# A pairwise-interaction tower: the short block of z on both halves of the rows, beside 64-row products, and a new order of the pieces

## The chip, the core and the metric

The kernel runs on one core of a Trainium2 chip. The metric is the device time in microseconds (us) of one execution, the median of several runs. All data are float32.

## What is computed

2048 samples, 32 features each. Each feature id picks a row of 64 numbers from its own table, so a sample has x of 32 x 64. From it come 32 row sums and 496 pair values x_i K_ij x_j, which with 16 dense numbers enter three dense layers.

```python
def _L0_rec_ref(x, kernels):
    ...
    z = jnp.sum(x, axis=-1)
    xi = x[:, II, :]
    xj = x[:, JJ, :]
    outer = jnp.einsum('bpd,pde,bpe->bp', xi, kernels, xj)
    return jnp.concatenate([z, outer], axis=1)
...
e = jnp.stack([tbl_0[ids[:, 0]], tbl_1[ids[:, 1]], ...], axis=1)
z = _L0_rec_ref(e, L0_rec_kernels)
h = jnp.concatenate([z, dense_ctx], axis=1)
h = jnp.maximum(h @ W_top1 + b_top1, 0.0)
h = jnp.maximum(h @ W_top2 + b_top2, 0.0)
y = h @ W_top3
```

## The kernel before, in words

The samples are cut into 8 batches (q = 0 to 7) of 256, two tiles of 128. Two features make a stage, so there are 16 stages; stage a holds one feature in the upper 64 rows and one in the lower 64 rows of `x_t`. These two halves of the rows of TensorE's array are called sides here: side 0 is rows 0 to 63, side 1 is rows 64 to 127.

A batch has 64 steps, in the order of `STEPS`. A step fills one of three product buffers `m_ps` (`MR = 3`) in PSUM and is then multiplied by VectorE. There are two kinds, 32 of each:

- An even step E0 to E31 (`multiply`, lines 633 and 635): four matmuls, two per side, with 64 rows of K as weights and 256 samples moving. VectorE's product (line 475) goes to `prod`. After every second even step TensorE adds up the products of an earlier pair with `sel` (`reduce`, line 663).
- A turned step T0 to T31 (`multiply_turned`, line 649): one matmul per side, with x as weights and 512 columns of K moving. VectorE's product (line 500) goes to `turned_act` or `turned_dve`; the sums over 64 are then made by ScalarE (line 409, sixteen small instructions a step) or, for the steps in `BY_VECTOR`, by VectorE itself (line 508, one instruction).

A step may begin when the product three steps earlier is finished (`prod_ready`). The last matmul of a step signals `step_done`, for which VectorE waits.

Between the steps TensorE does the pieces of the tower, each of them placed ahead of or behind an even step by the hand-written table `PLACED`, and each through the one buffer `tr` in PSUM: ScalarE must have copied a piece out (`tr_kept`) before the next may fill `tr`. The pieces of a batch are: "x" (line 553), eight transposes of two stages each for the next batch or for later stages of the same one; "xsum" (line 559), the transposes of the 32 row sums; "t" (line 567), those of the turned sums; "h1" 0 to 3 (line 572), the four chunks of the first layer; "h2" 0 and 1 (line 586), the second; and "y" (line 594), the third. Chunks belong to the batch before the one in whose steps they stand. The fifth number of a row in `PLACED` says how many steps later ScalarE copies the piece.

A chunk of h1 is five matmuls over the blocks of z: two of even pairs, two of turned pairs, and the short block (`ZSHORT`), of whose 128 rows only 48 carry values: 32 row sums and 16 dense numbers.

GpSimd gathers the table rows (line 310), four gathers a stage, and from batch 1 on also adds the two halves of each gathered row (`halve`, line 293), four gathers behind. A transposition "x" waits for that (`x_halved`), since `gathered` and `x_half` are rings.

In the last batch h1 is computed in the product buffers instead (`layer1_of_last`).

Of the kernel before, what the change touches and what calls it, by code (L numbers as in the profile page):

```python
# [20 lines left out]
MR = 3  # L21
# [24 lines left out]
BY_VECTOR = [_i in (1, 5, 6, 10, 12, 16, 18, 21, 23, 26, 28, 30) for _i in range(NT)]  # L46
# [5 lines left out]
for _a in range(STAGES):  # L52
# [6 lines left out]
    if _a % COLS == COLS - 1:  # L59
# [29 lines left out]
for _what, _i in STEPS[0]:  # L89
# [13 lines left out]

QUADS_OF_BLOCK = 16
# [7 lines left out]
ZLAST = SUM_ROWS + DENSE  # L112

# [71 lines left out]
VECTOR_SUMS_BEHIND = (1, 3, 5, 6, 7, 8, 9, 12, 13, 16, 17, 22, 25, 31)  # L185


def dlrm_tower(nc, ids, tables, kmat, dense_t, w1, b1, w2, b2, w3, out):
# [6 lines left out]
    with ctx:  # L195
# [122 lines left out]
        def _(sp):  # L318
# [14 lines left out]
            for q in range(NQ):  # L333
# [3 lines left out]
                sp.dma_start(z_sb[SUM_ROWS:ZLAST, q % 2, ZSHORT, :], dense_t[:, q * QB:(q + 1) * QB]).then_inc(dense_loaded[q % 2], 16)  # L337
# [8 lines left out]
        def _(act):  # L346
# [188 lines left out]
        def _(pe):  # L535
# [20 lines left out]
            def sums_of_x(q):  # L556
                pe.wait_ge(x_summed, (q + 1) * STAGES)
                for t in range(TILES):
                    last = nc.tensor.transpose(tr[0:SUM_ROWS, 0, t * P:(t + 1) * P], z_nat[:, q % 2, t, :], ident[:])
                last.then_inc(tr_filled, 1)  # L560

            def sums_of_turned(q):
# [5 lines left out]
                last.then_inc(tr_filled, 1)  # L568

# [28 lines left out]
            def fill(what, q, n):  # L598
# [3 lines left out]
                free_tr(what, q, n)  # L602
# [176 lines left out]
```

## Time and profile before

| | |
|---|---|
| median of 3 runs | 815.76 us (815.51 to 815.84) |
| the profiled execution, its own time | 816.48 us |
| its span, first to last instruction | 814.7 us |
| TensorE busy | 768.5 us (94%) |
| VectorE busy | 722.7 us (89%) |
| ScalarE busy | 682.0 us (84%) |
| GpSimd busy | 607.1 us (75%) |
| DMA engines, mean of the last 36 of 40 slices | one tenth or less |

The profile was taken in one execution. PE is TensorE's matmuls, PEld its weight loads, DVE VectorE, ACT ScalarE, POOL GpSimd. A float32 matmul of the program stands as two passes in the rows, so an even step has eight rows, a turned step four, a chunk of h1 ten. The time of a piece of TensorE's work is read here from the start of its first row to the start of the first row of the next piece, since the rows' own ends overlap.

### The profile page before, as it was taken

How to read it: one execution, taken by the hardware profiler on the slowest of the kernel's cores; microseconds unless marked ns; L12 is line 12 of the kernel's file. 1: busy time of each engine (PE TensorE's matmuls, PEld its weight loads, DVE VectorE, ACT ScalarE, POOL GpSimd, SP SyncE). 2: the span in 40 equal slices, each digit the busy share in tenths (PEclk: the TensorE clock that was granted, in tenths of full speed). 3: DMA queues.
4: the chain of work that ended last, by engine and by line, in shares of the span. 5: the costliest groups of instructions: out<-in, count | busy, mean ns of one | idle time of the engine just before them, and what ended most of it. 6: DMA issues, size and time to landing. Idle time of an engine off the chain costs nothing.

```text
span 814.7 us, 20371 instructions
## 1 busy us (share of the span) xinstructions
PE 768.5 (94%) x6000; PEld 451.0 (55%) x6000; DVE 722.7 (89%) x684; ACT 682.0 (84%) x5282; POOL 607.1 (75%) x966
## 2 busy tenths in 40 slices
PE   0389989999999999999999999999999999999998
PEld 0245445565655655565556556555565656565556
DVE  0269999989999899989999899999999899998992
ACT  1049897899879997899888998799978998889983
POOL 6776888888888887888868887888868888682000
PEclk9889999999999999999999999999999999999999
DMA  4545111111111111111111111111111111110000
GB/s 135 162 148 166 27 26 24 26 24 26 25 27 25 24 26 21 27 25 24 26 20 24 26 23 23 25 24 26 24 21 25 25 25 26 20 25 8 1 2 1
DMA packets 20014, 28.74 MB, mean 35 GB/s; under 512 B 9024, under 2 KB 9664, under 8 KB 19008
## 3 DMA queue, kind: packets, MB, share of 16 engines
q0 software_dynamic: 16384, 16.81, 10.7%
q1 hardware_dynamic: 3520, 10.63, 3.9%
q8 instruction: 48, 0.79, 0.4%
q14 instruction: 62, 0.51, 0.2%
HBM read 27.40 MB, written 0.01 MB: 34 GB/s over the span
## 4 chain that ended last, share of the span: by engine, by line
PE 79%; POOL 8%; DMA 6%; issue 3%; DVE 2%; ACT 1%; DVEq 0%; POOLq 0%
PE m_ps L649 24%; PE m_ps L633 24%; PE acc L663 13%; PE tr L572 8%; POOL gathered L310 7%; DMA gathered<-in_tbl,idx 6%; PE tr L553 4%; PE tr L586 3%; PE m_ps L572 1%; DVE prod L475 1%; POOL x_half L293 1%; ACT turned_act L409 1%; PE m_ps L635 1%; DVE turned_act L500 1%; PE tr L567 0%
## 5 line engine op out<-in xcount | busy, mean ns | idle before, releaser
L409 ACT ACTIVATE turned_act<-turned_act 128x64 f32<-128x64 f32 x2560 | 611.9, 244 | 2.7 <-DVE turned_act L500 2.6
L310 POOL DMA_INDIRECT gathered<-in_tbl,idx x512 | 489.4, 956 | 101.1 <-issue 76.6
L409 ACT ACTIVATION_READ_ACCUMULATOR turned_act<-turned_act 128x1 f32 x2560 | 488.3, 191 | 0.0
L475 DVE TENSOR_TENSOR prod<-m_ps,x_t 128x1024 f32<-128x1024 f32 x256 | 307.5, 1214 | 21.2 <-PE m_ps L635 20.3
L633 PE MATMUL m_ps<-x_t,k_sb 64*128 64x256 f32 x1024 | 269.1, 389 | 4.2 <-DVE turned_dve L500 2.6
L635 PE MATMUL m_ps<-x_t,k_sb 64*128 64x256 f32 x1024 | 269.4, 390 | 0.0
L649 PE MATMUL m_ps<-k_sb,x_t 64*128 64x512 f32 x1024 | 257.1, 609 | 1.3 <-DVE turned_dve L500 0.7
L633 PEld LDWEIGHTS m_ps<-x_t,k_sb 64*128 64x128 f32 x1024 | 184.4, 188 | 112.4 <-issue 73.7
L500 DVE TENSOR_TENSOR turned_act<-m_ps,gathered 128x1024 f32<-128x1024 f32 x160 | 192.5, 1215 | 13.9 <-PE m_ps L649 6.0
L635 PEld LDWEIGHTS m_ps<-x_t,k_sb 64*128 64x128 f32 x1024 | 184.2, 188 | 0.0
L293 POOL TENSOR_TENSOR x_half<-gathered 128x32 f32<-128x32 f32 x448 | 117.1, 262 | 30.0 <-DVE z_nat L459 20.8
L663 PE MATMUL acc<-prod,sel 128*32 128x256 f32 x2048 | 138.1, 387 | 0.6 <-DVE prod L475 0.5
L649 PEld LDWEIGHTS m_ps<-k_sb,x_t 64*128 64x128 f32 x1024 | 90.8, 186 | 74.5 <-issue 62.9
L500 DVE TENSOR_TENSOR turned_dve<-m_ps,gathered 128x1024 f32<-128x1024 f32 x96 | 117.1, 1219 | 7.8 <-issue 2.4
L508 DVE TENSOR_REDUCE z_turned<-turned_dve 128x16 f32<-128x1024 f32 x96 | 115.9, 1208 | 0.0
L353 ACT ACTIVATE x_t<-tr 128x512 f32<-128x512 f32 (+1 forms) x72 | 39.2, 545 | 69.5 <-PE tr L553 68.9
L663 PEld LDWEIGHTS acc<-prod,sel 128*32 128x32 f32 x2048 | 53.5, 109 | 66.1 <-issue 26.3
L553 PE MATMUL tr<-ident,gathered 128*128 128x128 f32 x256 | 45.0, 294 | 36.4 <-DMA gathered<-in_tbl,idx 34.7
L572 PE MATMUL tr<-z_sb,w_sb 128*128 128x256 f32 x280 | 67.9, 389 | 0.0
L553 PEld LDWEIGHTS tr<-ident,gathered 128*128 128x128 f32 x256 | 27.2, 143 | 66.2 <-issue 31.5
L572 PEld LDWEIGHTS tr<-z_sb,w_sb 128*128 128x128 f32 x280 | 50.9, 190 | 19.7 <-issue 14.0
L450 DVE TENSOR_REDUCE z_nat<-gathered 128x4 f32<-128x256 f32 x16 | 6.6, 412 | 32.1 <-DMA gathered<-in_tbl,idx 32.1
(36 smaller groups left out, 152.8 us busy)
## 6 DMA issues: line engine op xcount, KB each, us to landing
gathered<-in_tbl,idx POOLq DMA_INDIRECT x512, 2.5
k_sb<-in_kmat SPq DMA_DIRECT2D x7, 1024.0 KB, 4.9
w_sb<-in_w SPq DMA_DIRECT2D x1, 1280.0 KB, 9.0
k_sb<-in_kmat SPq DMA_DIRECT2D x2, 256.0 KB, 3.2
k_sb<-in_kmat SPq DMA_DIRECT2D x1, 512.0 KB, 5.0
w_sb<-in_w SPq DMA_DIRECT2D x1, 512.0 KB, 10.9
idx<-in_ids SPq DMA_DIRECT2D x1, 256.0 KB, 2.7
z_sb<-in_dense_t SPq DMA_DIRECT2D x8, 16.0 KB, 1.8
```

The source lines that it names most:

```text
L293: nc.gpsimd.tensor_tensor(x_half[:, G % HR, t, f, :], at[:, 0:D // 2], at[:, D // 2:D], ALU.add).then_inc(x_halved, 1)
L310: nc.gpsimd.indirect_dma_start(out=gathered[:, t, G % GR, f * D:(f + 1) * D], out_offset=None, in_=tables[2 * (STAGES - 1 - a) + f], in_of ...
L409: last = nc.scalar.activation(row, row, ACT.Copy, accum_out=z_turned[:, q % 2, t, 16 * c + n:16 * c + n + 1])
L475: nc.vector.tensor_tensor(prod[:, r % PR, :, :].rearrange("p u (e n) -> p u e n", e=2), m_ps[:, p % MR, :, :].rearrange("p u (e n) -> p u ...
L500: nc.vector.tensor_tensor(to, m_ps[:, p % MR, :, :], other, ALU.mult).then_inc(prod_ready, 1)
L508: nc.vector.tensor_reduce(z_turned[:, q % 2, t, 16 * c:16 * c + 16], turned_dve[:, (q * NTD + RANK[i]) % BD, :, :].rearrange("p f (u n) -> ...
L553: last = nc.tensor.transpose(tr[:, c, t * P:(t + 1) * P], gathered[:, t, (G + c) % GR, :], ident[:])
L572: last = nc.tensor.matmul(to, w1_sb[:, b, n * P:(n + 1) * P], z_sb[:, q % 2, b, :], start=(begin and b == blocks[0]), stop=(end and b == b ...
L633: nc.tensor.matmul(m_ps[:, p % MR, 0, n * QB:(n + 1) * QB], k_sb[0:D, at + n, :], x_t[0:D, slot(q, a0), :], start=True, stop=True)
L635: last = nc.tensor.matmul(m_ps[:, p % MR, 1, n * QB:(n + 1) * QB], k_sb[D:P, at + n, :], x_t[D:P, slot(q, a1), :], start=True, stop=True)
L649: last = nc.tensor.matmul(m_ps[:, p % MR, f, :], x_t[f * D:(f + 1) * D, slot(q, m), t * P:(t + 1) * P], k_sb[f * D:(f + 1) * D, at:at + CO ...
L663: last = nc.tensor.matmul(acc[c * 32:c * 32 + 32, 0:QB], sel[:, 30 - 2 * row:62 - 2 * row], prod[:, (q * NE + e) % PR, u, n * QB:(n + 1) * ...
```

## The change

The short block of z and its weights are put on both sides: rows 0 to 47 and rows 64 to 111 hold the same. The dense numbers are loaded twice, "xsum" gets for each tile a second matmul that writes the 32 sums to rows 64 to 95, and ScalarE copies them with a second instruction. A chunk's short block becomes one 64-row matmul (`short_block`), on side 0 for chunks 0 and 2, where it comes last, and on side 1 for chunks 1 and 3, where it comes first (`open_chunk`) and is issued ahead of the reduction that stands before the rest of the chunk. Between the two, the steps issue side 1 first (`sides = (1, 0)`).

In the last batch the short blocks of the four chunks are issued one behind the other, on alternate sides.

The order is new: both tables of turned steps, the places of all pieces and their copies, 13 instead of 12 turned steps summed by VectorE, and where those sums stand.

```diff
-BY_VECTOR = [_i in (1, 5, 6, 10, 12, 16, 18, 21, 23, 26, 28, 30) for _i in range(NT)]
+BY_VECTOR = [_i in (1, 4, 6, 9, 13, 15, 16, 18, 20, 23, 25, 29, 31) for _i in range(NT)]
...
-TURNED_LATER = [0, 1, 3, 5, 5, 7, 8, 8, 9, 11, 11, 11, 12, 12, 14, 14, 15, 16, 16, 17, 17, 20, 21, 22, 22, 24, 24,
+TURNED_LATER = [1, 1, 1, 2, 3, 5, 5, 6, 8, 8, 9, 12, 12, 13, 14, 14, 16, 16, 18, 18, 18, 19, 21, 21, 22, 24, 24,
...
-    ("x", 8, BEHIND, 5, 1),
+    ("x", 8, BEHIND, 3, 1),
...
-    ("xsum", 0, AHEAD, -3, 0),
+    ("xsum", 0, AHEAD, -4, 1),
-    ("h1", 0, BEHIND, 9, 2),
-    ("h1", 1, AHEAD, 12, 1),
-    ("h1", 2, AHEAD, 14, 2),
-    ("h1", 3, BEHIND, 17, 0),
+    ("h1", 0, BEHIND, 5, 4),
+    ("h1", 1, BEHIND, 7, 3),
+    ("h1", 2, BEHIND, 15, 1),
+    ("h1", 3, BEHIND, 17, -1),
...
-                sp.dma_start(z_sb[SUM_ROWS:ZLAST, q % 2, ZSHORT, :], dense_t[:, q * QB:(q + 1) * QB]).then_inc(dense_loaded[q % 2], 16)
+                for side in (0, D):
+                    sp.dma_start(z_sb[side + SUM_ROWS:side + ZLAST, q % 2, ZSHORT, :], dense_t[:, q * QB:(q + 1) * QB]).then_inc(dense_loaded[q % 2], 16)
...
+                nc.scalar.activation(z_sb[D:D + SUM_ROWS, q % 2, ZSHORT, :], tr[D:D + SUM_ROWS, 0, :], ACT.Copy).then_inc(tr_kept, 1)
...
+                    last = nc.tensor.matmul(tr[D:D + SUM_ROWS, 0, t * P:(t + 1) * P], z_nat[:, q % 2, t, :], ident[:], start=True, stop=True)
...
+            def short_block(q, n, to, begin, end):
+                side = D * (n % 2)
+                return nc.tensor.matmul(to, w1_sb[side:side + D, ZSHORT, n * P:(n + 1) * P], z_sb[side:side + D, q % 2, ZSHORT, :],
+                                        start=begin, stop=end)
+
+            def open_chunk(what, q, n):
+                free_tr(what, q, n)
+                short_block(q, n, tr[:, 0, :], True, False)
...
-                    layer1(q, n, tr[:, 0, :], range(NZ), True, True).then_inc(tr_filled, 1)
+                    if n % 2 == 0:
+                        layer1(q, n, tr[:, 0, :], range(ZSHORT), True, False)
+                        short_block(q, n, tr[:, 0, :], False, True).then_inc(tr_filled, 1)
+                    else:
+                        layer1(q, n, tr[:, 0, :], range(ZSHORT), False, True).then_inc(tr_filled, 1)
...
+                        sides = (1, 0) if what[0] == "h1" and what[2] % 2 == 0 else (0, 1)
...
-            layer1_of_last((NB - 1, ZSHORT), False, False)
+            layer1_of_last((NB - 1,), False, False)
+            for n in range(H1 // P):
+                short_block(LAST, n, m_ps[:, n // 2, n % 2, 0:QB], False, False)
```

What stands in a row on TensorE around chunks 0 and 1 of a batch in the middle, before (the lines' names are those of the list above; `acc` is a reduction, `tr<-z_sb` a chunk; an even step is four rows of 633 and 635):

```order
L663 MATMUL acc<-prod,sel 32x256 x8
L572 MATMUL tr<-z_sb,w_sb 128x256 x5
L649 MATMUL m_ps<-k_sb,x_t 128x512 x2
L633 MATMUL m_ps<-x_t,k_sb 128x256
L635 MATMUL m_ps<-x_t,k_sb 128x256
...
L663 MATMUL acc<-prod,sel 32x256 x8
L553 MATMUL tr<-ident,gathered 128x128 x4
L649 MATMUL m_ps<-k_sb,x_t 128x512 x6
L572 MATMUL tr<-z_sb,w_sb 128x256 x5
```

The same place after the change, where line 589 is the four full blocks of a chunk, 580 a short block, 670 turned steps (two matmuls each), 656 even steps (four each) and 684 a reduction:

```order
L684 MATMUL acc<-prod,sel 32x256 x8
L589 MATMUL tr<-z_sb,w_sb 128x256 x4
L580 MATMUL tr<-z_sb,w_sb 128x256
L670 MATMUL m_ps<-k_sb,x_t 128x512 x4
L656 MATMUL m_ps<-x_t,k_sb 128x256 x4
L670 MATMUL m_ps<-k_sb,x_t 128x512 x2
L656 MATMUL m_ps<-x_t,k_sb 128x256 x4
L580 MATMUL tr<-z_sb,w_sb 128x256
L684 MATMUL acc<-prod,sel 32x256 x8
L589 MATMUL tr<-z_sb,w_sb 128x256 x4
```

Between the two short blocks stand five steps (T5, T6, E6, T7, E7). Chunks 2 and 3 stand in the same way around four steps (E16, T16, T17, E17).

On VectorE the run of five steps that stood between a reduction and the next one before, T5, E8, T6, T7, E9, and its sums:

```order
L500 TENSOR_TENSOR turned_dve<-m_ps,gathered 128x1024
L475 TENSOR_TENSOR prod<-m_ps,x_t 128x1024
L508 TENSOR_REDUCE z_turned<-turned_dve 128x16
L500 TENSOR_TENSOR turned_dve<-m_ps,gathered 128x1024
L500 TENSOR_TENSOR turned_act<-m_ps,gathered 128x1024
L475 TENSOR_TENSOR prod<-m_ps,x_t 128x1024
```

And VectorE's rows for the run between the short blocks of chunks 0 and 1 after the change: T5, T6, E6, the sum of T6, T7, E7 and E8 (507 is a turned product, 482 an even one, 515 a turned sum):

```order
L507 TENSOR_TENSOR turned_act<-m_ps,gathered 128x1024
L507 TENSOR_TENSOR turned_dve<-m_ps,gathered 128x1024
L482 TENSOR_TENSOR prod<-m_ps,x_t 128x1024
L515 TENSOR_REDUCE z_turned<-turned_dve 128x16
L507 TENSOR_TENSOR turned_act<-m_ps,gathered 128x1024
L482 TENSOR_TENSOR prod<-m_ps,x_t 128x1024 x2
```

The two turned products have moved together to the head of the run.

The third place is the start of a batch on TensorE, up to "x" 8, the transposition of stages 8 and 9. Before, where the first row is "x" 4 of that batch, nine steps and three reductions stand ahead of the last row (rows of even steps are left out):

```order
L553 MATMUL tr<-ident,gathered 128x128 x4
L633 MATMUL m_ps<-x_t,k_sb 128x256
L635 MATMUL m_ps<-x_t,k_sb 128x256
...
L649 MATMUL m_ps<-k_sb,x_t 128x512 x2
...
L663 MATMUL acc<-prod,sel 32x256 x8
L553 MATMUL tr<-ident,gathered 128x128 x4
L649 MATMUL m_ps<-k_sb,x_t 128x512 x2
...
L663 MATMUL acc<-prod,sel 32x256 x8
L567 MATMUL tr<-ident,z_turned 128x128 x4
...
L663 MATMUL acc<-prod,sel 32x256 x8
L553 MATMUL tr<-ident,gathered 128x128 x4
```

After (560 is "x", 575 is "t"):

```order
L656 MATMUL m_ps<-x_t,k_sb 128x256 x8
L684 MATMUL acc<-prod,sel 32x256 x8
L560 MATMUL tr<-ident,gathered 128x128 x4
L670 MATMUL m_ps<-k_sb,x_t 128x512 x6
L575 MATMUL tr<-ident,z_turned 128x128 x4
L656 MATMUL m_ps<-x_t,k_sb 128x256 x4
L670 MATMUL m_ps<-k_sb,x_t 128x512 x2
L656 MATMUL m_ps<-x_t,k_sb 128x256 x4
L684 MATMUL acc<-prod,sel 32x256 x8
L560 MATMUL tr<-ident,gathered 128x128 x4
```

Eight steps and two reductions now stand ahead of "x" 8, one of each fewer.

## Rows read from the trace of the kernel before

**Rows 1.** Stretches between two times, busy us (instructions) of each engine:

```profile
core 0: us, PE busy (x) PEld busy (x) DVE busy (x) ACT busy (x) POOL busy (x), PEclk, DMA share, GB/s
324.88:419.46 94.58, 94.58 (x751) 56.17 (x750) 89.88 (x85) 84.82 (x660) 77.99 (x129) 1.00 0.13 24
132.80:230.31 97.51, 95.13 (x753) 55.97 (x749) 91.54 (x86) 85.89 (x672) 85.11 (x140) 1.00 0.13 25
...
148.26:230.31 82.05, 82.05 (x635) 48.51 (x635) 76.77 (x72) 75.35 (x592) 71.63 (x117) 1.00 0.13 26
```

**Rows 2.** Chain that ended last, 159 to 265 us: start us, us, what:

```profile
159.21 2.36 PE tr L572 x10
...
206.10 1.92 PE tr L586 x8
...
252.79 1.00 PE acc L663 x16
253.79 2.36 PE tr L572 x10
...
259.94 0.59 PE tr L553 x4
```

**Rows 3.** Timeline of TensorE around a run of five steps: start us, us, instruction:

```profile
342.65 1.13 PE L649 MATMUL m_ps<-k_sb,x_t 64*128 64x512 f32 x4
343.61 0.38 PE L633 MATMUL m_ps<-x_t,k_sb 64*128 64x256 f32 x1
343.62 0.38 PE L635 MATMUL m_ps<-x_t,k_sb 64*128 64x256 f32 x1
343.83 0.38 PE L633 MATMUL m_ps<-x_t,k_sb 64*128 64x256 f32 x1
...
344.48 1.88 PE L649 MATMUL m_ps<-k_sb,x_t 64*128 64x512 f32 x8
346.24 0.48 PE L633 MATMUL m_ps<-x_t,k_sb 64*128 64x256 f32 x1
...
347.30 1.07 PE L663 MATMUL acc<-prod,sel 128*32 128x256 f32 x16
```

**Rows 4.** Timeline of VectorE for the same five steps:

```profile
343.83 1.23 DVE L500 TENSOR_TENSOR turned_dve<-m_ps,gathered 128x1024 f32<-128x1024 f32 x1
344.97 1.21 DVE L475 TENSOR_TENSOR prod<-m_ps,x_t 128x1024 f32<-128x1024 f32 x1
```

**Rows 5.** Timeline of TensorE around "y" and "xsum":

```profile
406.46 1.07 PE L663 MATMUL acc<-prod,sel 128*32 128x256 f32 x16
407.35 0.41 PE L594 MATMUL tr<-h_sb,w_sb 128*1 128x64 f32 x16
...
410.47 0.39 PE L559 MATMUL tr<-ident,z_nat 128*32 128x128 f32 x2
410.79 0.48 PE L633 MATMUL m_ps<-x_t,k_sb 64*128 64x256 f32 x1
```

**Rows 6.** Timeline of TensorE in batch 1, idle time before in brackets:

```profile
146.00 1.07 PE L663 MATMUL acc<-prod,sel 128*32 128x256 f32 x16
148.26 0.66 PE L553 MATMUL tr<-ident,gathered 128*128 128x128 f32 x4 [1.19 <-POOL x_half L293]
```

**Rows 7.** Timeline of TensorE in batch 3, its "x" 8:

```profile
337.42 0.66 PE L553 MATMUL tr<-ident,gathered 128*128 128x128 f32 x4
```

**Rows 8.** Timeline of VectorE in batch 0:

```profile
45.52 1.23 DVE L475 TENSOR_TENSOR prod<-m_ps,x_t 128x1024 f32<-128x1024 f32 x1 [2.42 <-PE m_ps L635]
49.20 1.23 DVE L500 TENSOR_TENSOR turned_act<-m_ps,gathered 128x1024 f32<-128x1024 f32 x1 [2.46 <-DMA gathered<-in_tbl,idx]
```

**Rows 9.** Timeline of TensorE in the tail, the first 24 of the last chunks' passes:

```profile
798.58 5.35 PE L572 MATMUL m_ps<-z_sb,w_sb 128*128 128x256 f32 x24
```

**Rows 10.** Waits of POOL, 132.8 to 703.2 us: total us, times, longest:

```profile
POOL x_half L293 <- DVE z_nat L459: 20.8, 5, 4.9
```

**Rows 11.** Groups of instructions, ACT, 132.8 to 703.2 us: busy us, mean ns | idle before:

```profile
L409 ACT ACTIVATE turned_act<-turned_act 128x64 f32<-128x64 f32 x1927 | 460.5, 244 | 0.0
L371 ACT ACTIVATE z_sb<-tr 32x256 f32<-32x256 f32 x6 | 2.1, 358 | 0.0
```

More of the change, by code:

```diff
@@ L112 @@
 ZLAST = SUM_ROWS + DENSE
+assert ZLAST <= D
 K_LOADS = [4, 4, 8] + [16] * 7
@@ L632, in multiply, with multiply_turned @@
                 for n, (a0, a1, _, _) in enumerate(EVEN[e]):
-                    nc.tensor.matmul(m_ps[:, p % MR, 0, n * QB:(n + 1) * QB], k_sb[0:D, at + n, :], x_t[0:D, slot(q, a0), :],
-                                     start=True, stop=True)
-                    last = nc.tensor.matmul(m_ps[:, p % MR, 1, n * QB:(n + 1) * QB], k_sb[D:P, at + n, :], x_t[D:P, slot(q, a1), :],
-                                            start=True, stop=True)
+                    for f in sides:
+                        last = nc.tensor.matmul(m_ps[:, p % MR, f, n * QB:(n + 1) * QB], k_sb[f * D:(f + 1) * D, at + n, :],
+                                                x_t[f * D:(f + 1) * D, slot(q, (a0, a1)[f]), :], start=True, stop=True)
                 last.then_inc(step_done, 1)
-            def multiply_turned(q, i):
+            def multiply_turned(q, i, sides):
                 c, t = divmod(i, TILES)
@@ L667, in reduce @@
                         last.then_inc(reduced, 1)
+            sides = (0, 1)
+            opened = set()
             for q in range(NQ):
@@ L671, in _ @@
                     if kind == "turned":
-                        multiply_turned(q, n)
+                        multiply_turned(q, n, sides)
                         continue
-                    for what in AHEAD.get((q, n), ()):
+                    ahead, behind = AHEAD.get((q, n), ()), BEHIND.get((q, n), ())
+                    for what in ahead:
+                        if what[0] == "h1" and what[2] % 2:
+                            open_chunk(*what)
                         fill(*what)
-                    multiply(q, n)
+                        sides = (1, 0) if what[0] == "h1" and what[2] % 2 == 0 else (0, 1)
+                    multiply(q, n, sides)
+                    if behind and behind[0][0] == "h1" and behind[0][2] % 2:
+                        open_chunk(*behind[0])
+                        opened.add(behind[0])
                     if n % GROUP == GROUP - 1:
+                        sides = (0, 1)
                         if n >= GROUP:
@@ L681, in _ @@
                             reduce(q - 1, NG - 1)
-                    for what in BEHIND.get((q, n), ()):
+                    for what in behind:
+                        if what[0] == "h1" and what[2] % 2 and what not in opened:
+                            open_chunk(*what)
                         fill(*what)
+                        sides = (1, 0) if what[0] == "h1" and what[2] % 2 == 0 else (0, 1)
             reduce(LAST, NG - 1)
```

49 lines of the change are left out of this document (26 added, 23 removed).

## The prediction, written before the result was known

> **What bounds the kernel now.** I read the stretches first. In batch 3, from 324.88 to 419.46 us, TensorE is busy for all 94.58 us, VectorE for 89.88, ScalarE for 84.82, GpSimd for 77.99, all at the full clock [rows 1]. The chain that ended last says the same: it is a list of TensorE's pieces, and chunk 0 of h1 returns in it after 253.79 - 159.21 = 94.58 us [rows 2]. So from batch 2 on the period is the sum of what stands in TensorE's queue. Batch 1 is the exception: it takes 97.51 us of which TensorE is busy for 95.13 [rows 1], and the largest hole is the 1.19 us ahead of its "x" 8, which waits for GpSimd's halves [rows 6]; from there to the end of the batch the 82.05 us are dense again [rows 1]. Batch 0 is set by landing gathers and then by VectorE.
>
> Four prices for TensorE come out of the starts of the rows. A chunk of five blocks takes 2.36 us, h2 with four such matmuls 1.92 or so: a full block is 0.43 [rows 2]. A step is 0.86 (343.61 to 344.48; two in 344.48 to 346.24 with a little more) [rows 3]. The first step behind other work takes 0.96 (342.65 to 343.61), so entering a run of 64-row steps costs 0.10 [rows 3]; I take leaving it as 0.10 too, since a reduction of four passes deep lasts 1.00 [rows 2] where its passes fill 0.86. And the two sides run beside each other: line 633 starts at 343.61, line 635 at 343.62, and the second pass of 633 only at 343.83 [rows 3].
>
> VectorE is near enough to matter. A product follows another after 1.14 us (343.83 to 344.97) [rows 4], so in an unbroken run of steps TensorE, at 0.86 each, gains 0.28 a step on it and may be three steps ahead. A product begins 1.18 after the first row of its step (342.65 to 343.83). E9 was the fifth step of such a run and needed the product of E8, which ended at 344.97 + 1.21 = 346.18; E9 began at 346.24, where two turned steps end at 346.20, and had to pay the entry again (its first row is 0.48 instead of 0.38) [rows 3, 4]. So one such stop costs 0.04 to 0.10 plus 0.10. There are three a batch (E9, E17, E23), together some 0.55 us.
>
> **The change in a middle batch.** (1) Four full blocks go, 4 x 0.43 = 1.73 us. (2) Four 64-row matmuls of 0.43 come. If one on side 0 opens a run, the steps start on side 1, and one on side 1 closes it, both sides have the same load and a pair costs one slot: 2 x 0.43 = +0.85. Together -0.88.
>
> (3) "xsum" grows by two ordinary matmuls with 128 moving columns, two passes of half of 0.21 each, 0.43 in all. "y", sixteen passes on four groups of columns, takes 0.34 [rows 5], so different groups of columns do run side by side, and the transposes and the new matmuls write to different ones. No row shows the two kinds mixed. Bounds: +0.2 when they overlap ("xsum" is 0.32 now, 410.47 to 410.79 [rows 5]), +0.43 one behind the other, +0.7 if each change of kind costs an entry. I take +0.3, nearer to "y".
>
> (4) The number of runs of 64-row work goes from 19 to 20 a batch: +0.20. "y" no longer stands behind a reduction, where the reduction took 0.89 (406.46 to 407.35) [rows 5] instead of 1.00: +0.11; "xsum" now does and may get the same back. Net +0.06.
>
> (5) The old stops go, -0.55, and new ones come. In the run between chunks 0 and 1 the steps are issued side 1 first, so the last matmul of each step, which signals `step_done`, is on the side that carries the short block, and is 0.43 late. Count from the short block, with the entry 0.10: T5 starts at 0.10, T6 0.96, E6 1.82, T7 2.68, E7 3.54. VectorE gets T5 at 0.10 + 1.08 + 0.43 = 1.61, ends it at 2.83 and releases T7 0.06 later, at 2.89: a stop of 0.21. T6's product starts at 2.75, ends 3.96, frees E7 at 4.02, while TensorE is ready at 2.89 + 0.10 + 0.86 = 3.85: a stop of 0.17. With an entry each that is 0.58. The run between chunks 2 and 3 has four steps, E17 meets the first stop again: 0.31. E15, the fifth of a run without the delay, stops as E9 did: 0.16. New stops: 1.05. VectorE can't be ahead here: ahead of T5 it has waited for a reduction and four full blocks, about 2.9 us, and one more turned sum per batch (1.13 us) is spent where it has room: 94.58 - 89.88 = 4.7 us.
>
> Sum: 94.58 - 0.88 + 0.30 + 0.20 + 0.06 - 0.55 + 1.05 = **94.76 us**, +0.18 a batch. With the ends of (3) and (4) it is 94.6 to 95.3.
>
> ScalarE is given nothing that shows: it loses one turned step (sixteen times 244 ns [rows 11], in part overlapped), and gets one copy of about 358 ns [rows 11] a batch. The second dense load is a 16 KB transfer once a batch that waits for the same event as the first and is needed some twenty steps later. GpSimd waits for VectorE's sums up to 4.9 us in a batch now [rows 10], which is its slack; "x" 14 moves three even steps forward, so that wait moves with it. It would bind only under 94.58 - 4.9 = 89.7 us a batch.
>
> **Batch 0 and 1.** In batch 0 E2 moves behind the landing of stage 6. Before, VectorE had E3's product at 45.52 and then waited until 49.20 for stage 7 [rows 8]; now E2 fills that hole and E3 is left for later, and there is one turned sum more: batch 1 starts about 2 x 1.13 = 2.3 us later, at some 135.1. That is covered. "x" 8 of batch 1 can't run before 148.26 [rows 6], since GpSimd's gathers run without a break up to there and nothing moves them. TensorE now needs 10.7 us from the start of the batch to that point (before 337.42 - 324.88 = 12.5 in an undisturbed batch [rows 1, 7], less one step, 0.86, and one reduction, 1.00): it gets there at 145.8 and waits. But the step and the reduction that don't stand ahead of this wait any more have to be done behind it. From 148.26 to the end of the batch it takes 94.76 - 10.7 = 84.1 instead of 82.05 [rows 1]: **+2.0 us**, once.
>
> **Tail.** The 24 passes from 798.58 on [rows 9] lead the end. Four full short blocks become four 64-row ones in two slots: -0.85, and +0.20 for entering and leaving: -0.65.
>
> Total: +2.0 + 6 x 0.18 - 0.65 = +2.4. Batch 7 has the same steps and counts as one of the six. Against the profiled execution, 814.7 span and 816.48 in all, this is 818.9; the median lies 0.7 lower, so 815.76 + 2.4 = 818.2. I forecast **818.2 us**. In general the result is 815.8 + 7 x (P - 94.41), with P the period: 0.35 us of P decide over the sign.
>
> **Rivals.** A: the delay of 0.43 is not felt, because both sides of a step end together or the product is ready anyway. Then of the new stops only E7 and E15 stay as E9 was, 0.3 instead of 1.05: P = 94.0, 813.0 us. For it: the three stops before are only 0.04 to 0.10 deep. Against: the two sides start freely of each other [rows 3], and a queue of equal loads keeps its offset to the end of the run. Chance 0.22.
>
> B, slower: the short blocks don't hide. A product that starts alone on side 1 has to wait for the whole of the short block; the place is the head and the end of each of the two runs, the price up to 4 x 0.43 = 1.7 instead of 0.85 a batch, less 0.75 for stops that vanish with the offset: P between 94.9 and 95.6, 819 to 824 us. It decides as soon as more than 0.2 of each 0.43 is exposed. Against it stand the starts 0.01 apart of 633 and 635 [rows 3]. Chance 0.1.
>
> B2, slower: the passes start in the program's order, so that the first product on side 1 starts with the second pass of the short block, 0.21 behind its first. Half of each short block is exposed, 2 x 0.21 more a batch, while the offset and with it the stops shrink by about 0.2: P about 95.0, 820 us. Against it: the first pass of line 635 starts 0.21 ahead of the second pass of 633 [rows 3], although the program issues both passes of 633 in one matmul ahead of it. Chance 0.05. The Trainium skill, TensorE: Matmul & The Clock Gate, Part 3, What overlaps and what doesn't, says that matmuls start strictly in program order and that only weight loads are pulled ahead; by that rule this rival is what happens, and the trace of before does not agree.
>
> C: "xsum" at its dearest and every stop 0.1 deeper: P = 95.3, 822 us. Chance 0.08.
>
> D: the term of batch 1 is absent, because something between "x" 8 and the end of that batch has slack I don't see: 816.2 us. Against: 82.05 of 82.05 us busy. Chance 0.07.
>
> E: the change does not do what it says in its order, that is a copy by ScalarE (places of the fifth column) is late and TensorE waits for `tr`, 0.5 us a batch: 821 us. ScalarE idles 10 us a batch, so chance 0.05.
>
> My own forecast, P within 94.5 to 95.0, 816.5 to 820, has 0.43.
>
> **Range and chances.** 813.2 to 822.5 holds all but the ends of A, B and C. A measurement of this kernel tells 0.2% from no change, so the bounds are 814.1 and 817.4. Faster: most of A, 0.2. Same: the rest of A, D and the lower end of mine, 0.24. Slower: 0.56.
>
> **What will show it.** Right if the row after a chunk's four full blocks shows the short block and the first product of side 1 within 0.01 us of each other; if the period is 94.5 to 95.0 with stops ahead of T7, E7 and E17 and none ahead of E9 and E23; if "x" 8 of batch 1 still starts at 148.2 to 148.4 with an idle of 2 to 3 us before it, and the batch behind it takes 84 us; if "xsum" takes 0.5 to 0.75; and if the last chunks take 0.65 less. Wrong if no stop stands at T7 and E17 (A), if the first product starts 0.2 or more behind the short block (B or B2), or if batch 2 begins less than 1 us later than before (230.31).

## The result: 824.67 us, 8.9 us more than before

The changed kernel takes 824.67 us (median of 4 runs, 824.3 to 826.42), the kernel before 815.77 in the same comparison: a ratio of 1.0109, 95% interval 1.0097 to 1.0121. The direction was forecast, the size was not: 818.2 us was said, with a range up to 822.5. The profiled execution has a span of 822.6 us and 824.38 in all, 7.9 more than that of before (814.7 and 816.48).

Stretches of the changed kernel between the starts of its batches, busy us of each engine; they answer to [rows 1]:

```profile
core 0: us, PE busy (x) PEld busy (x) DVE busy (x) ACT busy (x) POOL busy (x), PEclk, DMA share, GB/s
135.67:233.00 97.33, 95.63 (x758) 56.52 (x754) 90.59 (x86) 81.03 (x626) 85.10 (x139) 1.00 0.13 25
148.11:233.00 84.89, 84.89 (x666) 50.46 (x666) 78.15 (x74) 72.33 (x562) 74.13 (x121) 1.00 0.13 25
328.56:424.11 95.55, 95.55 (x758) 56.53 (x755) 90.42 (x86) 81.43 (x630) 82.81 (x136) 1.00 0.13 26
```

TensorE is still the bound and still dense, but a middle batch takes 95.55 us instead of 94.58, and from "x" 8 of batch 1 to the end of that batch it takes 84.89 instead of 82.05. No other engine has moved near: VectorE has 90.42 of 95.55, GpSimd 82.81. So 7.9 us of span are: batch 2 begins at 233.00 instead of 230.31 (+2.69), five batches at +0.97 (+4.9), batch 7 +0.8, tail -0.5.

"xsum" in the timeline of TensorE of the changed kernel (start, length, line, operation), to be held against [rows 5], where it took 0.32 us:

```profile
507.06 1.07 PE L684 MATMUL acc<-prod,sel 128*32 128x256 f32 x16
508.06 0.29 PE L566 MATMUL tr<-ident,z_nat 128*32 128x128 f32 x1
508.28 0.41 PE L567 MATMUL tr<-ident,z_nat 128*32 128x128 f32 x2
508.62 0.28 PE L566 MATMUL tr<-ident,z_nat 128*32 128x128 f32 x1
508.83 0.41 PE L567 MATMUL tr<-ident,z_nat 128*32 128x128 f32 x2
509.17 0.49 PE L656 MATMUL m_ps<-x_t,k_sb 64*128 64x256 f32 x2
```

Line 566 is the transpose to rows 0 to 31, line 567 the new ordinary matmul to rows 64 to 95. They never run beside each other: an ordinary matmul starts 0.21 to 0.22 behind the transpose before it, the second transpose 0.34 behind the first of the two passes of the matmul before it, and the whole takes 509.17 - 508.06 = 1.10 us (the profile's own rounding), 0.78 more than before.

The run between chunks 0 and 1 of h1, TensorE and then VectorE:

```profile
345.52 0.48 PE L580 MATMUL tr<-z_sb,w_sb 64*128 64x256 f32 x1
345.53 0.69 PE L670 MATMUL m_ps<-k_sb,x_t 64*128 64x512 f32 x1
345.84 0.38 PE L580 MATMUL tr<-z_sb,w_sb 64*128 64x256 f32 x1
...
347.35 1.23 PE L656 MATMUL m_ps<-x_t,k_sb 64*128 64x256 f32 x7
348.39 0.69 PE L670 MATMUL m_ps<-k_sb,x_t 64*128 64x512 f32 x1
...
349.52 1.13 PE L656 MATMUL m_ps<-x_t,k_sb 64*128 64x256 f32 x8
350.49 0.59 PE L580 MATMUL tr<-z_sb,w_sb 64*128 64x256 f32 x2
...
```

```profile
347.11 1.23 DVE L507 TENSOR_TENSOR turned_act<-m_ps,gathered 128x1024 f32<-128x1024 f32 x1 [0.81 <-PE m_ps L670]
348.25 1.22 DVE L507 TENSOR_TENSOR turned_dve<-m_ps,gathered 128x1024 f32<-128x1024 f32 x1
...
```

The short block (line 580) and the first matmul of T5 (line 670) start 0.01 apart, so it is hidden. Its price is the lag: VectorE begins T5's product at 347.11, 1.58 after the first row instead of the 1.18 of [rows 3, 4]. T7 starts at 348.39, where E6, begun at 347.35, leaves one side free after 0.86, at 348.21: a stop of 0.18. E7 starts at 349.52, where T7 with its entry of 0.10 would be done at 349.35: 0.17. Each of the two waits for the product three steps earlier: T5's product ends at 347.11 + 1.23 = 348.34, 0.05 before T7 starts, and T6's at 348.25 + 1.22 = 349.47, 0.05 before E7.

Batch 1 of the changed kernel around "x" 8, and the first 24 passes of the last chunks, which answer to [rows 6] and [rows 9]:

```profile
145.34 1.07 PE L684 MATMUL acc<-prod,sel 128*32 128x256 f32 x16
148.11 0.66 PE L560 MATMUL tr<-ident,gathered 128*128 128x128 f32 x4 [1.70 <-POOL x_half L298]
...
806.99 3.62 PE L589 MATMUL m_ps<-z_sb,w_sb 128*128 128x256 f32 x16
810.54 1.13 PE L580 MATMUL m_ps<-z_sb,w_sb 64*128 64x256 f32 x8
811.60 0.44 PE L598 MATMUL tr<-ident,z_turned 128*128 128x128 f32 x2
```

"x" 8 is still tied to GpSimd, at 148.11 instead of 148.26. The 24 passes last from 806.99 to 810.54 + 1.13 = 811.67, 4.68 us where they were 5.35. From their first row to the start of the next piece it is 811.60 - 806.99 = 4.61 us, where it was 803.76 - 798.58 = 5.18, so 0.57 less.

### The profile page after: what moved, and what is told of

It is laid out like the page before. It is cut to its first block, busy times and chain, and to the rows that moved or that the text cites. A ratio compares the mean times of both kernels' runs of the same rounds, so it can differ in the third digit from the quotient of the medians.

```text
span 822.6 us, 20209 instructions
## 1 busy us (share of the span) xinstructions
PE 774.4 (94%) x6032; PEld 453.4 (55%) x6032; DVE 727.4 (88%) x692; ACT 655.9 (80%) x5034; POOL 607.2 (74%) x966
## 4 chain that ended last, share of the span: by engine, by line
PE 83%; POOL 6%; DMA 6%; issue 3%; DVE 2%; ACT 0%; DVEq 0%; POOLq 0%
PE m_ps L656 26%; PE m_ps L670 25%; PE acc L684 14%; PE tr L589 7%; DMA gathered<-in_tbl,idx 6%; POOL gathered L315 6%; PE tr L560 4%; PE tr L603 3%; PE tr L580 1%; DVE prod L482 1%; PE m_ps L589 1%; PE tr L567 1%; DVE turned_dve L507 1%; POOL x_half L298 0%; PE tr L575 0%
## 5 line engine op out<-in xcount | busy, mean ns | idle before, releaser
L416 ACT ACTIVATE turned_act<-turned_act 128x64 f32<-128x64 f32 x2432 | 581.8, 245 | 23.4 <-DVE turned_act L507 23.2
L416 ACT ACTIVATION_READ_ACCUMULATOR turned_act<-turned_act 128x1 f32 x2432 | 466.3, 192 | 0.0
L656 PE MATMUL m_ps<-x_t,k_sb 64*128 64x256 f32 x2048 | 280.9, 391 | 4.8 <-DVE prod L482 2.1
L656 PEld LDWEIGHTS m_ps<-x_t,k_sb 64*128 64x128 f32 x2048 | 195.5, 188 | 103.0 <-issue 58.7
L507 DVE TENSOR_TENSOR turned_dve<-m_ps,gathered 128x1024 f32<-128x1024 f32 x104 | 126.7, 1218 | 3.1 <-PE m_ps L670 0.9
L515 DVE TENSOR_REDUCE z_turned<-turned_dve 128x16 f32<-128x1024 f32 x104 | 125.9, 1211 | 0.0
L589 PE MATMUL tr<-z_sb,w_sb 128*128 128x256 f32 x224 | 55.8, 392 | 0.0
L589 PEld LDWEIGHTS tr<-z_sb,w_sb 128*128 128x128 f32 x224 | 40.2, 189 | 15.9 <-issue 11.5
L603 PE MATMUL tr<-h_sb,w_sb 128*128 128x256 f32 x112 | 27.9, 392 | 0.0
L603 PEld LDWEIGHTS tr<-h_sb,w_sb 128*128 128x128 f32 x112 | 20.1, 189 | 7.9 <-issue 5.8
```

Of the source, the lines that this page charges most:

```text
L416: last = nc.scalar.activation(row, row, ACT.Copy, accum_out=z_turned[:, q % 2, t, 16 * c + n:16 * c + n + 1])
L507: nc.vector.tensor_tensor(to, m_ps[:, p % MR, :, :], other, ALU.mult).then_inc(prod_ready, 1)
L515: nc.vector.tensor_reduce(z_turned[:, q % 2, t, 16 * c:16 * c + 16], turned_dve[:, (q * NTD + RANK[i]) % BD, :, :].rearrange("p f (u n) -> ...
L589: last = nc.tensor.matmul(to, w1_sb[:, b, n * P:(n + 1) * P], z_sb[:, q % 2, b, :], start=(begin and b == blocks[0]), stop=(end and b == b ...
L603: last = nc.tensor.matmul(to, w2_sb[:, c, n * P:(n + 1) * P], h1_sb[:, c, :], start=(c == 0), stop=(c == H1 // P - 1))
L656: last = nc.tensor.matmul(m_ps[:, p % MR, f, n * QB:(n + 1) * QB], k_sb[f * D:(f + 1) * D, at + n, :], x_t[f * D:(f + 1) * D, slot(q, (a0, ...
```

## Experiments

**My theory after the result** was: the excess over the forecast is "xsum" (its mixed kinds), the stops stem from the lag of the side with the short block, and batch 1 pays for what no longer stands ahead of GpSimd. **Rivals**: VectorE's thirteenth sum, ScalarE's second copy or the second load set the period; or the short block isn't hidden at all. The columns "xsum" and batch (a middle one) are from each kernel's trace, the times are medians.

| kernel | order | short block | "xsum" | batch | time |
|---|---|---|---|---|---|
| before | old | full | 0.32 | 94.58 | 815.8 |
| new_order_alone | the change's | full | 0.32 | 94.87 | 820.06 |
| sums_all_matmuls | the change's | 64 rows | 0.54 | 94.88 | 821.34 |
| sums_grouped | the change's | 64 rows | 0.88 | 95.33 | 824.07 |
| after (the change) | the change's | 64 rows | 1.10 | 95.55 | 824.67 |
| side0_first | the change's | 64 rows | 1.10 | 95.60 | 824.81 |
| old_order_new_block | old | 64 rows, unpaired | 1.10 | 95.35 | 821.19 |
| new_block_new_order | own, no stops | 64 rows, unpaired | 0.54 | 94.32 | 812.13 |
| old_block_again | own, no stops | full | 0.32 | 94.11 | 812.41 |
| paired_mixed_again | own, no stops | 64 rows, paired | 1.10 | 94.03 | 811.45 |
| paired_again | own, no stops | 64 rows, paired | 0.54 | 93.36 | 807.21 |

old_order_new_block, side0_first and new_block_new_order ran on another chip, on which the kernel before took 816.41 us; the ratios given below are to the kernel before on the same chip.

### What "xsum" costs

Both matmuls of "xsum" made ordinary ones:

```diff
                 for t in range(TILES):
-                    nc.tensor.transpose(tr[0:SUM_ROWS, 0, t * P:(t + 1) * P], z_nat[:, q % 2, t, :], ident[:])
+                    nc.tensor.matmul(tr[0:SUM_ROWS, 0, t * P:(t + 1) * P], z_nat[:, q % 2, t, :], ident[:], start=True, stop=True)
                     last = nc.tensor.matmul(tr[D:D + SUM_ROWS, 0, t * P:(t + 1) * P], z_nat[:, q % 2, t, :], ident[:], start=True, stop=True)
```

> The changed kernel, but the side-0 half of "xsum" is made with ordinary matmuls as well, so its four matmuls are of one kind. Theory (the excess of a batch sits in the changes between transpose and ordinary matmul inside "xsum", which lasts 1.10 us): "xsum" falls to 0.50-0.55 us, the batch from 95.55 to about 95.0, the time by 7 x 0.55 = 3.9 to 820.8 us. Rival V (VectorE's thirteenth sum, ScalarE's second copy or the second dense load sets the period): no more than 0.5 us of change, 824.2-824.7. Rival W (four passes simply cost 0.22 each one behind the other, whatever their kind): "xsum" 0.9, 823.3 us.

Measured: 821.34 us (821.03 to 821.75), ratio to before 1.0067 (1.0051 to 1.0084). Its "xsum" in the timeline of TensorE:

```profile
506.41 1.07 PE L684 MATMUL acc<-prod,sel 128*32 128x256 f32 x16
507.29 0.27 PE L566 MATMUL tr<-ident,z_nat 128*32 128x128 f32 x1
507.31 0.27 PE L567 MATMUL tr<-ident,z_nat 128*32 128x128 f32 x1
...
507.84 0.49 PE L656 MATMUL m_ps<-x_t,k_sb 64*128 64x256 f32 x2
```

Lines 566 and 567 now start 0.02 apart, and four matmuls take 0.54 us. V falls, and W too. The batch is 0.67 shorter: 0.56 inside "xsum", and 0.11 in the reduction ahead of it, which lasts 0.88 us up to "xsum" (506.41 to 507.29), where it lasts 1.00 in the change (507.06 to 508.06), with a transpose behind it. The second run of the pair has the transposes in front and the matmuls behind:

```diff
                 for t in range(TILES):
                     nc.tensor.transpose(tr[0:SUM_ROWS, 0, t * P:(t + 1) * P], z_nat[:, q % 2, t, :], ident[:])
+                for t in range(TILES):
                     last = nc.tensor.matmul(tr[D:D + SUM_ROWS, 0, t * P:(t + 1) * P], z_nat[:, q % 2, t, :], ident[:], start=True, stop=True)
```

> The changed kernel, but "xsum" issues its two transposes first and then its two ordinary matmuls: one change of kind inside it instead of three. Theory: two changes of about 0.10 us fewer, "xsum" 0.9 instead of 1.10, the batch 95.35, the time 824.7 - 7 x 0.2 = 823.3 us. Rival V: 824.7, nothing. Rival W (no price for a change of kind, each piece waits for the one before): "xsum" stays at 1.1, 824.7 us.

Measured: 824.07 us (823.2 to 824.65), ratio 1.0102 (1.0085 to 1.0119), batch 95.33:

```profile
507.78 0.39 PE L566 MATMUL tr<-ident,z_nat 128*32 128x128 f32 x2
508.10 0.62 PE L568 MATMUL tr<-ident,z_nat 128*32 128x128 f32 x4
508.66 0.49 PE L657 MATMUL m_ps<-x_t,k_sb 64*128 64x256 f32 x2
```

508.66 - 507.78 = 0.88: two changes of kind fewer are worth 0.22 a batch. The trace says it to the hundredth; the medians (0.6 us apart, 1.5 by seven batches) agree only roughly, and the ranges overlap.

### What the order costs, and batch 1

The kernel before, with nothing but the tables of the change (`BY_VECTOR`, `TURNED_FIRST`, `TURNED_LATER`, `PLACED`, `FIRST_AHEAD`, `KEEP_Z_LATER`, `VECTOR_SUMS_BEHIND`):

> The kernel before with its full short block and its old "xsum", and only the tables of the order from the change (sums by VectorE, places of the tower's pieces, turned sums, transposes of batch 0). Theory: the order alone has stops of its own and leaves "x" 8 of batch 1 earlier in its batch: batch 94.76, batch 2 begins about 2.7 us later than at 230.31, together +3.9: 819.7 us. Rival (the order was only made to fit the new short block and is otherwise neutral): 815.8 us. Rival (without the lag of side 1 all stops go): period 94.3, 815.8 + 2.7 - 2 = 816.5 us.

Measured: 820.06 us (819.94 to 821.69), ratio 1.0057 (1.0041 to 1.0074); batch 94.87, "x" 8 of batch 1 at 147.72 behind a hole of 1.91 us, batch 2 at 231.93. A middle batch, same columns as above:

```profile
326.80:421.66 94.86, 94.86 (x754) 56.01 (x750) 90.32 (x86) 80.99 (x629) 82.80 (x137) 1.00 0.14 25
```

By the medians the order alone costs 4.3 of the 8.9 us, by the spans of the profiled executions 3.5 (818.2 against 814.7): 0.29 a batch, and 1.6 once. The forecast of 2.7 for batch 1 came from the change; against it, "x" 8 is 0.39 earlier here (147.72 against 148.11), and the rest of the batch is 0.68 shorter, as every batch is (94.87 against 95.55). With the 64-row block and the cheap "xsum" on top, the batch is 94.88: in this order the new block gives 0.88, and it takes 0.11 for "xsum" (0.22 more inside it, 0.11 less in the reduction ahead of it) and some 0.78 for stops by the lag, so that nothing is left. The traces of the two kernels bear the 0.78 out: the five steps between chunks 0 and 1 have 0.4 more of stops and entries, the four between chunks 2 and 3 have 0.3, and 0.1 stands behind T20. So the 0.97 by which a batch of the change is longer than before is 0.29 of order, 0.67 of mixed kinds around "xsum" and 0.01 of all the rest.

To price the anchor by itself, the kernel before with "x" 8 moved in batch 1 alone:

```diff
     for _what, _n, _where, _e, _ in PLACED:
+        if (_what, _n, _q) == ("x", 8, 1):
+            _where, _e = AHEAD, 4
```

> The kernel before, with one placement moved: in batch 1 alone, "x" 8 stands ahead of step E4 instead of behind E5, so E4, E5 and a reduction have to be done behind the point at which GpSimd has the halves, 148.2 us. Theory (what doesn't stand ahead of that wait is pushed behind it): "x" 8 of batch 1 stays at 148.2, the idle ahead of it grows from 1.2 to about 4 us, batch 2 begins 2.9 us later, the time is 815.8 + 2.9 = 818.7 us; all later batches keep 94.58. Rival (batch 1 has slack elsewhere that gives it back): 815.8-816.3 us.

Measured: 821.57 us (820.32 to 822.26), ratio 1.0072 (1.0055 to 1.0089); the profiled execution has a span of 818.5, 3.8 more than before, and batch 2 begins 3.81 later (234.12). By the medians it is 5.8 more; the other three runs took 821.0 to 822.3 us, at a mean granted clock of 0.987 to 0.992, and what is read here is the profiled execution's 3.8. The direction is the theory's, the size isn't. The stretch from 148 to 150 us (same columns as above) and the timeline of TensorE:

```profile
148.00:150.00 2.00, 2.00 (x10) 1.52 (x10) 0.00 (x0) 1.75 (x12) 1.80 (x4) 0.50 0.11 24
```

```profile
147.51 0.70 PE L555 MATMUL tr<-ident,gathered 128*128 128x128 f32 x4 [3.26 <-POOL x_half L295]
148.14 0.79 PE L635 MATMUL m_ps<-x_t,k_sb 64*128 64x256 f32 x1
...
148.73 0.63 PE L635 MATMUL m_ps<-x_t,k_sb 64*128 64x256 f32 x1
...
149.16 0.63 PE L635 MATMUL m_ps<-x_t,k_sb 64*128 64x256 f32 x1
...
151.66 1.07 PE L665 MATMUL acc<-prod,sel 128*32 128x256 f32 x16
```

After a hole of 3.26 us the granted clock is 0.50, the lower of the two levels (1.2 GHz), and the passes of E4 stand 0.43 apart instead of 0.21. E4 and E5 take 151.66 - 148.14 = 3.52 us where 0.10 + 2 x 0.86 + 0.10 = 1.9 was due. So behind "x" 8 there are 4.56 us more (234.12 - 147.51 = 86.61 against 82.05): the 2.9 of the theory and 1.6 of clock; GpSimd was 0.75 early, which leaves 3.81. The kernel with four ordinary matmuls shows the same in small: it reaches "x" 8 sooner, waits 2.37 us, and then

```profile
148.00:150.00 2.00, 2.00 (x8) 1.16 (x9) 0.30 (x1) 1.51 (x10) 1.82 (x3) 0.52 0.20 33
```

which costs it about 1.6 us (85.86 us from "x" 8 at 147.83 to the end of the batch at 233.69, 0.97 more than in the change, with a middle batch 0.67 shorter). In the change itself (hole of 1.70), in the new order alone (1.91) and with grouped sums (2.14) the granted clock stayed at 1.00.

### Whether the short block hides

The changed kernel with the old tables:

> The changed kernel (64-row short blocks, sums in all four matmuls of "xsum" as in the change, second dense load, second copy by ScalarE), but with the tables of the order of the kernel before. Theory (block and order are separate accounts; the block saves 0.88 and its mixed "xsum" costs 0.79 a batch, and in the old order only one or two stops are deepened by the lag of side 1): batch 94.6-94.9, batch 2 begins within 0.3 us of 230.3, tail 0.6 shorter: 815.5-817.5, best 816.2 us. Rival (the short blocks need the new order to hide, otherwise each 0.43 stands alone): batch 95.4, 821 us. Rival (all of the +8.9 is in the block's parts, copies and loads): 822-824 us.

Measured: 821.19 us (820.73 to 821.87), ratio 1.0061 (1.0044 to 1.0078), batch 95.35. My theory fell, the first rival gave the number: 95.35 - 94.58 = 0.77 is about the 0.78 of "xsum", and the four short blocks saved nothing. Where it goes stands in the timeline of TensorE behind chunk 0:

```profile
351.05 0.48 PE L578 MATMUL tr<-z_sb,w_sb 64*128 64x256 f32 x1
351.06 0.69 PE L668 MATMUL m_ps<-k_sb,x_t 64*128 64x512 f32 x1
...
354.26 1.07 PE L682 MATMUL acc<-prod,sel 128*32 128x256 f32 x16
```

The block starts with the first product (351.05, 351.06), hidden as it seems. But the three steps T8, E10 and E11 last until the reduction at 354.26, 3.21 us instead of 0.10 + 3 x 0.86 + 0.10 = 2.78. The side that carries the block is 0.43 behind, and a reduction over all rows has to wait for it. In the old order other work stands between chunk 0 and chunk 1, and no short block on the other side closes this run. In this kernel an unpaired 64-row block costs as much as a full one, 0.43.

The changed kernel with side 0 always issued first:

```diff
-                        sides = (1, 0) if what[0] == "h1" and what[2] % 2 == 0 else (0, 1)
+                        sides = (0, 1)
```

> The changed kernel, but every step issues side 0 first, also behind a short block on side 0. Theory: a matmul of side 1 that stands in the queue behind one of side 0 can't pass it, so the first step behind the short block begins 0.43 late on both sides; in exchange nothing lags, and the stops ahead of T7, E7 and E17 go: batch 95.4-95.7, 824-826 us. Rival (the sides run freely of each other whatever the order of issue): the lag goes and the block stays hidden, the stops of some 0.8 a batch vanish: batch 94.8, 819.5 us.

Measured: 824.81 us (824.69 to 824.97), ratio 1.0104 (1.0087 to 1.0121), batch 95.60. The number fits my theory, the mechanism doesn't, and the rival's fits no better. TensorE and VectorE in the same run as above:

```profile
345.55 0.48 PE L580 MATMUL tr<-z_sb,w_sb 64*128 64x256 f32 x1
345.56 0.69 PE L670 MATMUL m_ps<-k_sb,x_t 64*128 64x512 f32 x1
...
346.08 1.88 PE L670 MATMUL m_ps<-k_sb,x_t 64*128 64x512 f32 x7
...
348.44 0.69 PE L670 MATMUL m_ps<-k_sb,x_t 64*128 64x512 f32 x1
```

```profile
347.15 1.23 DVE L507 TENSOR_TENSOR turned_act<-m_ps,gathered 128x1024 f32<-128x1024 f32 x1 [0.82 <-PE m_ps L670]
```

T5 starts at once, at 345.56, although the first matmul issued for it is on the occupied side. That one can only be among the rows from 346.08 on, when the block's second pass (345.87) has had its 0.21: the matmul issued later, on the free side, started 0.52 ahead of the one issued before it. The stops stay, too, and VectorE begins 1.59 behind the first row, as in the change (1.58). The last matmul of a step, which signals, is now on the free side, and still its signal comes only when the side with the block is through. The trace of this run has the times: the second pass of the signalling matmul begins at 346.09 and is 0.59 long (to 346.68), the second pass on the other side begins at 346.51 (to 347.10), and `step_done` rises at 347.13. So the lag is not made by the order in which the sides are issued: VectorE waits for one semaphore, and the semaphore rises when both halves are through.

### An order that fits

The rest of the loss should then be stops, pairs and the hole. Two kernels test it, both with four ordinary matmuls in "xsum" and with tables chosen so that by the prices of the rows no step of a middle batch waits for VectorE. The first was made before I knew of the pairs:

> The changed kernel with "xsum" in four ordinary matmuls and with other numbers in the tables of the order: 20 runs of 64-row work a batch as in the change, but by the prices of the rows (step 0.86, product 1.14 apart, signal of side 1 late by 0.43) no step waits for VectorE in a middle batch, GpSimd's halves are waited for 0.5 us at most in batch 1. Theory (all that is left of the loss beside "xsum" is stops and the hole of batch 1): batch 93.5 instead of 94.88, batch 2 begins 5-6 us earlier than in the kernel with four ordinary matmuls: 806-808 us. Rival (ScalarE or GpSimd comes to bind once TensorE is faster): batch 94.2-94.6, 812-815 us.

Measured: 812.13 us (812.0 to 812.6), ratio 0.995 (0.9934 to 0.9967), batch 94.32: faster than before, but 0.8 a batch longer than its sum. In its timeline the reductions behind the two runs that a short block opens come late, as in the old order:

```profile
334.30 0.48 PE L578 MATMUL tr<-z_sb,w_sb 64*128 64x256 f32 x1
...
337.51 1.07 PE L682 MATMUL acc<-prod,sel 128*32 128x256 f32 x16
```

3.21 us for three steps again, and 2 x 0.43 = 0.86 is about what was missing. The second kernel keeps the pairs together; its table differs from the change's in such lines:

```diff
-    ("x", 8, BEHIND, 3, 1),
+    ("x", 8, BEHIND, 5, 1),
...
-    ("t", 0, AHEAD, 2, -1),
-    ("h1", 0, BEHIND, 5, 4),
-    ("h1", 1, BEHIND, 7, 3),
+    ("t", 0, AHEAD, 4, 2),
+    ("h1", 0, BEHIND, 6, 0),
+    ("h1", 1, BEHIND, 7, 2),
```

> The paired order once more: on the chip of the run before, every kernel, the unchanged one too, took half as long again, with VectorE and ScalarE standing still for 7 to 17 us at places that have nothing to do with the program. Theory (pairs hide the short blocks, nothing stops): batch 93.4, batch 2 begins at about 229, 806-808 us. Rival (pairs don't matter, ScalarE or GpSimd sets the 0.8 us a batch that the earlier new order was longer than its sum): batch 94.2, 811-813 us.

Measured: 807.21 us (806.41 to 807.94), ratio 0.9891 (0.9876 to 0.9906), batch 93.36; 8.6 us less than the kernel before and 17.5 less than the change. A middle batch, and the run between chunks 0 and 1:

```profile
323.00:416.40 93.40, 93.40 (x760) 56.67 (x758) 90.70 (x86) 81.49 (x630) 81.51 (x135) 1.00 0.13 26
```

```profile
341.57 0.48 PE L578 MATMUL tr<-z_sb,w_sb 64*128 64x256 f32 x1
341.57 0.69 PE L668 MATMUL m_ps<-k_sb,x_t 64*128 64x512 f32 x1
...
344.26 0.38 PE L578 MATMUL tr<-z_sb,w_sb 64*128 64x256 f32 x1
...
344.78 1.07 PE L682 MATMUL acc<-prod,sel 128*32 128x256 f32 x16
```

The three steps take 344.78 - 341.57 = 3.21 us, as long as the unpaired run, but now with two short blocks in them. The run between chunks 2 and 3 (T16, E16, E17) also has three steps and lasts 3.21. With three steps in the run instead of four or five, the lag reaches no step that needs a buffer. The batch is 94.32 - 93.36 = 0.96 shorter than in the kernel without pairs, of which two pairs give 0.86. The hole ahead of "x" 8 of batch 1 is 1.16 us at the full clock. The same kernel with the change's "xsum":

> The paired order with the change's "xsum", transpose and ordinary matmul in turns. Theory: "xsum" 1.10 instead of 0.54 and the piece ahead of it up to 0.11 dearer, batch 94.0, 7 x 0.6 = 4.4 us more than the paired order: 811-812 us. Rival (the price shows only where VectorE or GpSimd is late anyway): less than 2 us more.

Measured: 811.45 us (811.42 to 811.67), ratio 0.9947 (0.9933 to 0.996), batch 94.03: +0.67 a batch and +4.2 in all, as in the order of the change. And the full block with an order of its own:

> The kernel before (full short block, two transposes in "xsum"), with tables of the order in which by the prices of the rows no step waits for VectorE. Theory (the block is worth 0.86 less the 0.22 of two more ordinary matmuls a batch where it is paired and has no stops): batch 94.0 instead of 94.58, some 3 us more than the paired order: 809.5-811 us. Rival (the new block is worth nothing even with an order of its own): the same time as the paired order.

Measured: 812.41 us (811.38 to 812.82), ratio 0.9956 (0.9943 to 0.997), batch 94.11. The time is 1.4 us over the range said; the batch is 0.1 over. Against new_block_new_order (94.32) the batch is 0.21 shorter, which is the 0.22 of "xsum": unpaired, the 64-row blocks are worth nothing in a fitting order either. Paired, the new block with ordinary matmuls is worth 94.11 - 93.36 = 0.75 a batch, or 0.97 without the 0.22 that its "xsum" costs more; the forecast had 0.88. The two kernels have different orders, so these figures hold for block and order together.

These last three kernels ran first on a chip where the kernel before, too, took 1231 us and VectorE and ScalarE stood still at odd places; the ratios to it were 0.9916 (paired), 0.9894 (with the change's "xsum") and 1.0089 (full block). Both paired kernels were faster than before there too, but the third was slower; nothing here rests on these runs, and why that chip stood still stays open.

## The prediction, point by point

**Right.** TensorE's queue is the bound and a batch is the sum of it. The short block starts 0.01 from the first product and a pair costs one slot (terms 1 and 2); rival B and B2 are out. By the Trainium skill, TensorE: Matmul & The Clock Gate, Part 3, What overlaps and what doesn't, B2 would have come true, since matmuls should start in program order; the trace of after disagrees as that of before did, pass by pass, with T5 at 345.53 ahead of the second pass of line 580 at 345.84. With side 0 first the disagreement is one of whole matmuls: T5's second matmul starts at 345.56 and its first at 346.08. The same section says that the matmul issued last also ends last, and there the runs agree in effect: with side 0 first, VectorE's start stayed at 1.59. The lag of 0.43 is felt, stops stand ahead of T7, E7 and E17 (0.18, 0.17 and 0.18, where 0.21, 0.17 and 0.21 were said) and none ahead of E9 and E23; rival A (0.22) is out. "x" 8 of batch 1 stays with GpSimd, and the batch behind it is P - 10.7: 95.55 - 10.7 = 84.85 against 84.89 measured; rival D is out. The 24 passes of the tail are 0.67 shorter by their busy time and 0.57 up to the next piece (0.65 forecast). Batch 1 began at 135.67 (135.1 forecast), and that was covered.

**Right, but for less than the whole reason.** I put the lag on the matmul that signals being on the side with the short block. In the change it is there, but that doesn't decide: with side 0 first the signalling matmul was on the free side, and the semaphore rose as late.

**Wrong: term (3), "xsum" +0.3.** It measured +0.78, above even the upper bound of 0.7. The two rows I leaned on, "y" on four groups of columns and the transposes in 0.32, are each of one kind; the row I lacked, kinds mixed, was the dear end. The bound "each change of kind costs an entry" was the true mechanism, and it belonged nearer to the middle. This, the term of "xsum", is the step that failed: 0.48 of the 0.79 by which P was missed (95.55 against 94.76).

**Too small: terms (4) and (5).** The reduction ahead of "xsum" did not get back what "y" got: it takes 0.11 more than with ordinary matmuls behind it. The forecast had counted on half of that, so 0.05 is missing. E15 begins at 371.87 behind two turned steps that began at 370.01:

```profile
370.01 1.88 PE L670 MATMUL m_ps<-k_sb,x_t 64*128 64x512 f32 x8
371.87 0.92 PE L656 MATMUL m_ps<-x_t,k_sb 64*128 64x256 f32 x6
```

They fill 1.72, so the stop is 0.14 and with the entry 0.24 instead of 0.16. Two stops of the new order were not in the forecast at all, behind T20 and at E31, the last step of the batch:

```profile
384.11 2.84 PE L670 MATMUL m_ps<-k_sb,x_t 64*128 64x512 f32 x12
386.88 0.66 PE L560 MATMUL tr<-ident,gathered 128*128 128x128 f32 x4
...
422.06 1.12 PE L656 MATMUL m_ps<-x_t,k_sb 64*128 64x256 f32 x8
423.11 0.42 PE L684 MATMUL acc<-prod,sel 128*32 128x256 f32 x4
```

T18, T19 and T20 take 2.77 us to "x", where 3 x 0.86 + 0.10 = 2.68 was due, and E31 takes 1.05 instead of 0.96: 0.09 each. With 0.48 + 0.05 + 0.08 this makes the 0.79. The one at T20 is missing in new_order_alone (2.68), the one at E31 is there too.

**What it did to the total.** 0.79 a batch enters five times in the middle batches, once in batch 1, and nearly whole in batch 7: 5.4 of the 5.5 us by which the profiled execution missed the forecast. The last 1.0 us is between profiled execution and median: before, the median was 0.7 lower; of the change it is 0.3 higher. Rival C had the mechanism ("xsum" at its dearest, stops deeper) and 0.08, with 95.3 and 822 us; the chance was too low, and the range ended where it ended.

**What I didn't ask.** That a short block needs its partner in the same run was in my sentence on terms 1 and 2 as a condition, and the change keeps it. But I didn't see that the change is an order for the pairs first of all, nor that the pairs, at five or four steps a run, buy 0.88 and pay some 0.78 of it back in stops.

## What to carry to other kernels

Work on half of the rows is free only if the other half gets as much before the next thing that needs all rows; otherwise it moves the wait to that thing, and rows that start together prove nothing about the run's end. Price a batch with the lag in it: a run short enough that no step in it needs a buffer back hides the lag, a longer one pays. And where two kinds of instruction are to be mixed on TensorE and no row shows the mix, give the dear end real weight, or make them of one kind.

## What the runs showed of the hardware

- Transposes and ordinary matmuls on different groups of columns don't overlap: in turns 1.10 us, in two groups 0.88, all ordinary 0.54, where ordinary ones start 0.02 apart. A change of kind costs about 0.11 (two fewer, 0.22 less).
- A matmul on one side of the rows passes one on the other that was issued earlier (in side0_first 345.56 against 346.08), but its signal doesn't: the semaphore rose at 347.13, 0.45 behind the end of its last pass, and VectorE's start stayed at 1.59 behind the step's first row.
- A 64-row matmul that has no partner on the other side between two pieces that need all rows costs 0.43, as much as a full one: three steps take 3.21 us instead of 2.78. With a partner the same three steps take 3.21 for both.
- TensorE's granted clock was 0.50 after a hole of 3.26 us and 0.52 after one of 2.37, and 1.00 after holes of 1.70, 1.91 and 2.14. Either drop cost about 1.6 us on top of the hole.
